# Weighing gathered expert results on ScalarE, and summing a tile's six by fewer and wider VectorE additions

## The reference

```
s    = sigmoid(xf @ Wr.T + br)                  # 32 experts in 8 groups
idx, w = the 6 best experts of the 4 best groups, their weights normalised, times 2.5
acc  = sum over experts e of gate[:, e] * (square(relu(xf @ W1[e].T)) @ W2[e].T)
g    = silu(square(relu(xf @ Ws1.T)) @ Ws2.T + acc)
out  = x + s * g
```

## Time and profile before

| | us |
|---|---|
| median of 3 runs (385.95 to 387.05) | 386.65 |
| the profiled execution, its own time | 382.94 |
| its span, first to last instruction | 381.1 |
| TensorE busy with products | 308.8 (81%) |
| VectorE busy | 269.4 (71%) |
| ScalarE busy | 240.6 (63%) |
| GpSimd busy | 221.0 (58%) |

### The profile page before, as it was taken

One profiled execution on the slowest core, in us unless ns is written; L12 is line 12 of the kernel. 1 busy time (PEld: TensorE's weight loads), 2 busy tenths in 40 slices (PEclk: granted clock), 3 DMA queues, 4 the chain that ended last, 5 costly groups with the idle time before them and its releaser, 6 DMA issues.

```text
span 381.1 us, 8188 instructions
## 1 busy us (share of the span) xinstructions
PE 308.8 (81%) x2716; PEld 234.7 (62%) x2716; DVE 269.4 (71%) x634; ACT 240.6 (63%) x383; POOL 221.0 (58%) x232
## 2 busy tenths in 40 slices
PE   0585886899996878789798888789797798799962
PEld 0353654667785757677575676676475477687841
DVE  4688889998955286647567564447855786699866
ACT  5878799555484676676686576796645653544432
POOL 1966889855877356454663646500076565666750
PEclk9998699899999899999999999999999899899997
DMA  7951160254773366364644646434597565567742
GB/s 262 400 177 58 21 214 24 87 169 137 241 253 101 95 171 206 113 193 126 193 140 132 205 131 211 143 113 136 180 320 223 151 181 150 174 168 207 204 110 83
DMA packets 38762, 62.89 MB, mean 165 GB/s; under 512 B 5026, under 2 KB 26690, under 8 KB 38722
## 3 DMA queue, kind: packets, MB, share of 16 engines
q1 hardware_dynamic: 31474, 42.57, 34.4%
q0 software_dynamic: 7248, 19.80, 18.2%
HBM read 46.66 MB, written 15.70 MB: 164 GB/s over the span
## 4 chain that ended last, share of the span: by engine, by line
PE 52%; DVE 16%; issue 9%; ACT 9%; DVEq 6%; another core or an unknown queue 3%; POOL 2%; ACTq 2%; DMA 1%
PE hp L947 5%; PE hp L945 4%; PE hp L946 4%; PE rot L909 4%; PE hp L932 4%; PE dp L1001 4%; PE dp L1004 4%; PE dp L1003 4%; DVE xs L1284 3%; DVEq L1286 3%; PE hp L934 3%; PE bp L892 3%; DVE hf L1260 2%; PE rot L960 2%
## 5 line engine op out<-in xcount | busy, mean ns | idle before, releaser
L607 POOL DMA_INDIRECT xgt<-xtab,ids x91 | 93.7, 1029 | 63.7 <-PE rot L909 36.3
L617 POOL DMA_INDIRECT wst<-ytab,slot x60 | 62.7, 1045 | 61.3 <-DMA ytab<-wst 27.1
L688 ACT ACTIVATE hf<-hf 128x512 f32<-128x512 f32 (+1 forms) x80 | 49.9, 623 | 72.1 <-DVE hf L1260 52.8
L1001 PE MATMUL dp<-wt,hhi 128*128 128x256 f16 x204 | 56.7, 278 | 5.2 <-ACT xs L722 2.9
L1277 DVE COPY wst<-rot 128x512 f32<-128x512 f32 (+1 forms) x35 | 23.7, 680 | 51.7 <-PE rot L962 37.9
L1004 PE MATMUL dp<-wt,hhi 128*128 128x256 f16 x204 | 56.6, 277 | 1.2 <-issue 1.2
L1003 PE MATMUL dp<-wt,hlo 128*128 128x256 f16 x204 | 56.6, 278 | 1.0 <-issue 1.0
L693 ACT ACTIVATE hhi<-hf 128x512 f16<-128x512 f32 (+1 forms) x80 | 49.9, 624 | 5.7
L945 PE MATMUL hp<-xh,wt 128*128 128x512 f16 (+1 forms) x148 | 51.1, 345 | 0.9 <-DVE hf L1260 0.6
L703 ACT ACTIVATE xgt<-rot 128x1024 f16<-128x1024 f16 (+1 forms) x46 | 46.1, 1002 | 7.8 <-remote 5.0
L947 PE MATMUL hp<-xh,wt 128*128 128x512 f16 (+1 forms) x148 | 50.9, 344 | 0.0
(11 more groups left out here) (174 smaller groups left out, 703.1 us busy)
## 6 DMA issues: line engine op xcount, KB each, us to landing
gate_bc<-gtab SPq DMA_DIRECT2D x48, 256.0 KB
ytab<-wst SPq DMA_DIRECT2D x45, 256.0 KB
wst<-in_wts SPq DMA_DIRECT2D x17, 512.0 KB, 5.6
xs<-in_x SPq DMA_DIRECT2D x4, 512.0 KB, 5.0
xgt<-in_x SPq DMA_DIRECT2D x4, 512.0 KB
out<-xgt SPq DMA_DIRECT2D x16, 128.0 KB
xtab<-xn SPq DMA_DIRECT2D x3, 512.0 KB, 3.1
xgt<-xtab,ids POOLq DMA_INDIRECT x91
```

Source lines behind the costliest of these rows:

```text
L607: nc.gpsimd.indirect_dma_start(xg[:, a % XRING, :, :].rearrange("p h d -> p (h d)"), None, xtab, bass.IndirectOffsetOnAxis(ids[:, a:a + 1] ...
L617: nc.gpsimd.indirect_dma_start(yk[:, n % KRING, :], None, ytab, bass.IndirectOffsetOnAxis(slot[:, n // K, n % K:n % K + 1], 0))\
L688: nc.scalar.activation(hf[:, k % HP, 0:width(k)], hf[:, k % HP, 0:width(k)], ACT.Square, scale=W_SCALE ** (-0.5 if gated else -1.0))
L1001: nc.tensor.matmul(o, hhi[:, k % HRING, hcols], hi, start=(e == 0 and q % 2 == 0), stop=False, skip_group_check=True)
```

## The change

ScalarE multiplies each gathered result by its weight, in place (`weigh_result`), two in a unit as the additions were before. VectorE adds a routed tile at once, one unit behind its last weighing: results 0 to 2 plus results 3 to 5 in one addition of 768 columns, then three additions of 256 columns. `yk` has 12 places instead of 6, so that one tile can be weighed while another is summed; gathers wait for ScalarE's weighing, and from the thirteenth on for VectorE's sum as well. `ysb` has five places instead of six, of which two lie in the tile `xn`, because `yk` takes their memory. Routed tiles are finished one unit later; the last three tiles are then finished in the order 4, 5, 15.

```diff
-YRING = 6
-KRING = 6
+YRING = 5
+YLATE = 3
+KRING = 12
...
-        ysb = late[:, 0:YRING]
-        hpre, hh = late[:, YRING], late[:, YRING + 1]
-        gvar, grstd = late[:, YRING + 2, 0], late[:, YRING + 2, 1]
+        hpre, hh = late[:, YLATE], late[:, YLATE + 1]
+        gvar, grstd = late[:, YLATE + 2, 0], late[:, YLATE + 2, 1]
...
+        y_early = xn[:, :, :].rearrange("p (n t) d -> p n t d", t=2)
+        ysb = lambda s, n: late[:, s, 0:n, :] if s < YLATE else y_early[:, s - YLATE, 0:n, :]
...
             if j in ROUTED:
-                whole = ADD_AT + K * (ROUTED.index(j) + 1) // 2
+                whole = ADD_AT + K * (ROUTED.index(j) + 1) // 2 + 1
...
             def gather_result(n):
                 if n >= AHEAD:
-                    pool.wait_ge(yk_used, n - AHEAD + 1)
+                    pool.wait_ge(yk_weighed, n - AHEAD + 1)
+                if n >= KRING:
+                    pool.wait_ge(yk_used, (n // K - KRING // K + 1) * K)
...
+            def weigh_result(n):
+                act.wait_ge(yk_landed[n % KRING], 16 * (n // KRING + 1))
+                act.wait_ge(wk_ready, n // K + 1)
+                nc.scalar.activation(yk[:, n % KRING, :], yk[:, n % KRING, :], ACT.Copy, scale=wk[:, n // K, n % K:n % K + 1])\
+                  .then_inc(yk_weighed, 1)
...
                 for c in BLOCKS:
                     if k == last_of[c] + 3:
                         leave_sum(c)
+                for n in range(adds_by(k - 1), adds_by(k)):
+                    weigh_result(n)
                 for j in finishing(k):
                     silu_sum(j)
...
-            def add(n):
-                j = ROUTED[n // K]
-                dve.wait_ge(yk_landed[n % KRING], 16 * (n // KRING + 1))
-                if n == 0:
+            def add(i):
+                j, at = ROUTED[i], i * K % KRING
+                dve.wait_ge(yk_weighed, K * (i + 1))
+                if i == 0:
                     dve.wait_ge(shared_out, len(shared_no))
-                nc.vector.scalar_tensor_tensor(acc[:, j, :], yk[:, n % KRING, :], wk[:, n // K, n % K:n % K + 1],
-                                               acc[:, j, :], ALU.mult, ALU.add).then_inc(yk_used, 1)
+                nc.vector.tensor_tensor(yk[:, at:at + 3, :], yk[:, at:at + 3, :], yk[:, at + 3:at + K, :], ALU.add)
+                dve.drain()
+                nc.vector.tensor_tensor(yk[:, at, :], yk[:, at, :], yk[:, at + 1, :], ALU.add)
+                nc.vector.tensor_tensor(acc[:, j, :], acc[:, j, :], yk[:, at + 2, :], ALU.add)
+                dve.drain()
+                nc.vector.tensor_tensor(acc[:, j, :], acc[:, j, :], yk[:, at, :], ALU.add).then_inc(yk_used, K)
                 dve.drain()
...
-                for n in range(adds_by(k - 1), adds_by(k)):
-                    add(n)
+                for i in range(adds_by(k - 2) // K, adds_by(k - 1) // K):
+                    add(i)
```

More of the change, by code:

```diff
@@ L298, in build @@
         sm_ready = sem("sm_ready")
+        wk_ready = sem("wk_ready")
+        yk_weighed = sem("yk_weighed")
         yk_used = sem("yk_used")
@@ L471, in store_y @@
                     sp.dma_start(ytab[own[0] * P:(own[-1] + 1) * P, :].rearrange("(a p) d -> p a d", p=P),
-                                 ysb[:, v % YRING, 0:len(own), :]).then_inc(y_stored[v % YRING], 16)
+                                 ysb(v % YRING, len(own))).then_inc(y_stored[v % YRING], 16)
             def load_again(c):
@@ L716, in leave_slots @@
                     act.wait_ge(y_stored[v % YRING], 16 * (v // YRING))
-                nc.scalar.activation(ysb[:, v % YRING, 0:len(own), :], rot[:, bank_of["leave", k, h], 0:len(own), :], ACT.Copy).then_inc(y_act, 1)
+                nc.scalar.activation(ysb(v % YRING, len(own)), rot[:, bank_of["leave", k, h], 0:len(own), :], ACT.Copy).then_inc(y_act, 1)
             def leave_sum(c):
@@ L1249, in slot_gates @@
                 dve.drain()
-                nc.vector.tensor_reduce(wk[:, i:i + n, :], e, AX.X, ALU.add)
+                nc.vector.tensor_reduce(wk[:, i:i + n, :], e, AX.X, ALU.add).then_inc(wk_ready, n)
             def relu(k):
@@ L1276, in leave_slots @@
                     dve.wait_ge(wlo_pool, POOL_STEPS)
-                nc.vector.tensor_copy(ysb[:, v % YRING, 0:len(own), :], rot[:, bank_of["leave", k, h], 0:len(own), :]).then_inc(y_out, 1)
-            def add(n):
-                j = ROUTED[n // K]
-                dve.wait_ge(yk_landed[n % KRING], 16 * (n // KRING + 1))
-                if n == 0:
-                    dve.wait_ge(shared_out, len(shared_no))
-                nc.vector.scalar_tensor_tensor(acc[:, j, :], yk[:, n % KRING, :], wk[:, n // K, n % K:n % K + 1],
-                                               acc[:, j, :], ALU.mult, ALU.add).then_inc(yk_used, 1)
+                nc.vector.tensor_copy(ysb(v % YRING, len(own)), rot[:, bank_of["leave", k, h], 0:len(own), :]).then_inc(y_out, 1)
+            def add(i):
+                j, at = ROUTED[i], i * K % KRING
+                dve.wait_ge(yk_weighed, K * (i + 1))
+                if i == 0:
+                    dve.wait_ge(shared_out, len(shared_no))
+                nc.vector.tensor_tensor(yk[:, at:at + 3, :], yk[:, at:at + 3, :], yk[:, at + 3:at + K, :], ALU.add)
[4 more added lines that the diff above has]
+                nc.vector.tensor_tensor(acc[:, j, :], acc[:, j, :], yk[:, at, :], ALU.add).then_inc(yk_used, K)
                 dve.drain()
```

## The result

| | runs | median, us | range |
|---|---|---|---|
| before | 4 | 386.85 | 385.95 to 390.21 |
| after | 4 | 393.04 | 391.48 to 393.85 |

The ratio is 1.0139, 95% interval 1.0071 to 1.0207. The forecast was 385.2 with a range of 382.6 to 389.0, and 0.48 for faster: wrong in sign, and outside the range. The profiled execution after has its own time 393.85 and a span of 391.9.

The account below looks back on a forecast made before the run. TensorE's 2.68 us units were the tail's floor, VectorE slower only where finishes come unit after unit. Terms -0.9 + 1.1 - 1.3 + 1.0 - 0.3 = -0.4, or -2.4; middle -1.4 gave 381.5 profiled, 385.2 unprofiled, range 382.6 to 389.0.

Parts of the forecast that it names:

- VectorE's prices: Additions on VectorE: 0.96 us for one of 768 columns, 2.4 us for a tile's whole sum.
- ScalarE's price: One weighing of a 128x256 result on ScalarE: 0.50 us, the middle of 0.402 and 0.591.
- its cover: ScalarE's work in a unit, 2.5 to 2.85 us against TensorE's 2.68: thin, but weighing costs nothing while it holds.
- (a): First gathers: relu 54 no longer stands behind them, so TensorE gains 0.9 us.
- (b): Unit 65: tile 9's sum delays relu 65 and the dense sum's copy, +1.1 us; TensorE's wait 2.9 becomes about 4.
- (c): Units 67 to 77: TensorE's three waits for relus go, -1.3 us; -3.5 if VectorE's queue itself decides.
- (d): The end: tile 14's sum delays the last low half, +1.0 us; tile 15's sum replaces two pairs, -0.3.
- Five places: Five places for stored results instead of six: costs nothing, at the worst some tenths of a us.
- The carried-over difference: Unprofiled median 386.65 is 3.7 us above the profiled execution; added to the profiled forecast of 381.5.
- the bunch falls on the critical relus: Rival: 2.4 us stand before relu 65 and the last low half; +2.1 us, 388.7, chance 0.14.
- ScalarE stands at the gathers: Rival: ScalarE waits for gathered results, 0.15 us a unit over 28 units; +4 us, 390.6, chance 0.10.
- the sum for a queue that decides by itself: All four terms if relu 78 has no other wait than VectorE's queue: -2.4 us instead of -0.4.

Follow-up runs that it names:

- e1: The changed kernel, nothing edited, run again beside the kernel before in a quick (350 us) series: 354.17 against 350.64 us, 1.012.
- e3: The changed kernel, but VectorE adds each weighed result by itself, two in each unit; quick series: 347.04 us, 0.9908 of the kernel before.
- e14: e3 with the dense sum's copy first in unit 65 and gathers 11 ahead instead of 5; quick series: 0.9839 of the kernel before.
- e16: The changed kernel with the weighted additions of before on VectorE, twelve places, gathers 11 ahead, dense sum's copy first; quick series: 0.9925 of the kernel before.
- e2: The changed kernel's memory layout alone: additions, six gather places and finishing order as before, five places for stored results; quick series: 0.9976 of the kernel before.
- e5: The kernel before, nothing edited, against itself in a quick series: 351.0 us, 1.0042.
- e4: The changed kernel without weighing on ScalarE: VectorE does a tile's six weighted additions together; quick series: 1.0146 of the kernel before.
- e7: The changed kernel with gathers waiting for the weighing 11 results before instead of 5; quick series: 350.51 us, 1.0007 of the kernel before.
- e9: The changed kernel, wide additions kept, with the dense sum's copy first in unit 65 and gathers 11 ahead; late series: 1.0385 of the kernel before.
- e11: The same kernel as e16 (VectorE's weighted additions of before, twelve places, gathers 11 ahead, copy first) in a late series: 1.012 of the kernel before.
- e17: The changed kernel with the dense sum's copy first in unit 65, gathers 5 ahead; late series: 1.0071 of the kernel before.

## Why the prediction was wrong

**VectorE's prices, right.** Wide addition 0.958 (0.96), a tile's sum 339.42 - 337.09 = 2.33 us in e1 (2.4).

**ScalarE's price, right** (0.496 for 0.50), and so is what was said of its cover: e3, and e14 against e16, show the weighing there as a gain.

**(a) The first gathers, -0.9: not seen.** From the first gather to relu 56 the change is 0.2 us longer in e1 than in e2. Relus 53 to 55 do come earlier (relu 53 at 256.92 for 260.61), but relu 56 stands behind tile 6's sum, which waits for six results. The step took the first results as if each could still be used as it came.

**(b) Unit 65, +1.1: the right mechanism, mis-sized; +3.9.** Relu 65 came 3.94 us behind relu 64 (3.6 forecast) in e1. TensorE's stand grew by 1.5 us, near the forecast. What the sum left out is the clock: 2.8 us over 36 products, most of them at the lower level. I had read a low spell behind the shorter stand and put a further one into a rival only, at 1.2. In the quick series the kernel before has no low spell there and the change has one (e5 against e1 and e4), so the change brings all of it. In the first comparison the stand went from 2.9 to 5.6, of which late instructions are part: relu 65 waited another 2.25 us for its products.

**(c) Units 67 to 77, -1.3 to -3.5: right.** 30.65 to 29.57 us up to relu 77, and 3.0 us up to relu 79. The point from which I let the bunch decide ("where TensorE regains less than 1 us in units 67 to 77") was wrong: the relus of those units came 1.1 us closer together, and the bunch still won.

**(d) The end: the step that failed.** The place of the last low half, 5.8 behind relu 78, was about right (6.3 in e1; +1.3 behind relu 79, +1.2 forecast there). "Now tile 15's sum (2.4) replaces two pairs ...: 6.6, so -0.3" was wrong: 10.21 for 6.81 in e1, 8.88 for 6.91 in the first comparison. I priced the sum as work and forgot that it must wait for the last of six, while single additions use the time in which the results arrive. And the step "A gather still starts when the fifth result before it is used, now by ScalarE, some 0.7 us later in the unit" took that 0.7 as free. Weighings stand in ScalarE's queue behind a square that stands behind a relu that stands behind a sum, so a bunch stops the gathers, and GpSimd has next to nothing to catch up with: a gather takes 1.03 to 1.07 us and a gap of 0.30 (e2, e1), and two have to fit in a unit of 2.68. This second part is the smaller one, 1.3 of the 4.7 us (e7).

**Five places, right**: nothing (e2).

**The carried-over difference** of 3.7 us between the profiled and the other runs is inside the scatter of single runs: the kernel before ranges from 346.5 to 353.6 even in one quick series.

Of the rivals, "the bunch falls on the critical relus" was the right one, at 0.14, with +2.1 for a measured +3.5 us (e1). "ScalarE stands at the gathers" named the wrong hour: not +4 from the first gathers on (+0.2 up to relu 56 in e1), but a part of the late end. In the sum for a queue that decides by itself (-2.4), the mis-sized terms are (a) +1.1, (b) +2.8 and (d) +3.8 (+4.7 for a forecast of +1.2 - 0.3): that makes +5.3, and the table above has +5.4 for e1 against e2 (medians: 354.17 - 349.28 = +4.9).

**What stays open.** What makes TensorE's instructions late in some series. Each trace has 24 transfers of 16 KB of the instruction queue, and they took no longer in a late profile (1.05 us on average before and 1.12 after, first comparison) than in a quick one (1.10, e2 and e5). That a longer lead makes it worse rests on e9 and e11 in one series and e17 in another; e11 has that lead and no more "issue" waits than the kernel before (22.4 us), yet is at 1.012. Nor is it shown why e7 kept its clock.

## What to carry to other kernels

Fewer and wider instructions save an engine's time, but a sum of six is ready only with its sixth input: spread it where the results trickle in, above all at the end, and keep it from in front of the instruction on whose result another engine's copy waits. Before a stall is priced, ask what clock TensorE returns with: here the stand was 1.5 us longer and the products behind it cost 2.8 more. When work moves to another engine's queue, everything that was paced by it (here the gathers) inherits what stands ahead of it there; with single additions that was little (the last gather 2.7 us behind relu 79 for 2.0), with bunches it was more (5.4). The mend may be one line: the dense sum's copy at the head of its unit gave back the whole loss in a quick series, and left 0.7% in a late one.

## What the hardware showed that I hadn't expected

The same program took 350 us in some series and 387 in others, on one and the same chip, with TensorE's "issue" waits at 1.4 us in a quick profile and 22.4 in a late one; a change's worth differs between them (0.9837 and 1.0008; 0.9883 and 1.0385). A stand of TensorE of 3.0 us (e1), of 3.9 (e4) and of 2.9 in the first comparison's kernel before was followed by 1.2 GHz, one of 2.9 us in e7 was not (granted clock 0.57, 0.57, 0.63 and 1.00 over the 8, 8, 3.7 and 8 us that begin near its end).
